# Softmax attention inside an eight-layer model: the bf16 product that opens a score bank, issued half a unit ahead for one head of each pair

## The reference

```python
x = x + _L1_attn_a_ref(_layernorm(x, axis=-1), L1_attn_a_Wq, ...)

q = (x @ Wq.T + bq).reshape(b, s, h, dh)      # b = 1, s = 2048, h = 16, dh = 32
k = (x @ Wk.T + bk).reshape(b, s, h, dh)
v = (x @ Wv.T + bv).reshape(b, s, h, dh)
q = q * jnp.cos(rot)
k = k * jnp.sin(rot)
scores = jnp.einsum('bshd,bthd->bhst', q, k) / np.sqrt(dh).astype(np.float32)
scores = scores * spiral_weight[None, :, None, None]
attn = jax.nn.softmax(scores, axis=-1)
out = jnp.einsum('bhst,bthd->bshd', attn, v).reshape(b, s, d)
return out @ Wo.T + bo
```

## Time and profile before

| | |
|---|---|
| Time, median of 3 runs | 5405.37 us (5400.83 to 5413.63) |
| Profiled execution: its own time | 5397.6 us |
| Its span, first to last instruction | 5395.9 us |
| `attention_heads`, first exponential to the last group's end | 1285 to 2278 us of the span |
| of that, the three quarters which the change touches | 1285 to 2109 us |
| of that, the last quarter | 2109 to 2278 us |
| TensorE over the whole span | 4767.6 us busy, 88% |

### The profile page before, as it was taken

One profiled execution on the slowest core, in us unless ns is written; L12 is line 12 of the kernel. 1 busy time (PEld: TensorE's weight loads), 2 busy tenths in 40 slices (PEclk: granted clock), 3 DMA queues, 4 the chain that ended last, 5 costly groups with the idle time before them and its releaser, 6 DMA issues. The chain is left out here.

```text
span 5395.9 us, 66202 instructions
## 1 busy us (share of the span) xinstructions
PE 4767.6 (88%) x26222; PEld 2548.7 (47%) x26224; DVE 2412.7 (45%) x3331; ACT 1633.7 (30%) x2761; POOL 1532.6 (28%) x953
## 2 busy tenths in 40 slices
PE   7367997899999999967999869999999989589996
PEld 3133433333333333245666536666666654366663
DVE  7854778366666666634222223333333321332222
ACT  5414553212555546702111122222222210121110
POOL 1010000003777764012555401111111110045553
PEclk9688998999999999978999989999999999699998
DMA  2000000100000000044999720000000031459997
GB/s 70 0 2 19 6 0 2 33 0 1 1 1 1 1 1 1 3 165 115 246 253 254 170 76 25 29 30 30 30 22 30 24 105 62 169 163 253 245 254 201
DMA packets 237103, 417.66 MB, mean 77 GB/s; under 512 B 30992, under 2 KB 119056, under 8 KB 236816
## 3 DMA queue, kind: packets, MB, share of 16 engines
q1 hardware_dynamic: 179472, 270.89, 14.5%
q0 software_dynamic: 57344, 142.64, 12.2%
HBM read 297.53 MB, written 115.93 MB: 77 GB/s over the span
## 5 line engine op out<-in xcount | busy, mean ns | idle before, releaser
L2284 PE MATMUL linb_pr_ps<-lin_z,linb_wt 128*128 128x512 f32 x1536 | 679.3, 596 | 16.4 <-POOL linb_slope_own L2254 16.4
L1460 ACT ACTIVATE attc_prob<-attc_ps 128x512 f32<-128x512 f32 x1024 | 548.9, 597 | 438.2 <-PE attc_ps L1371 435.4
L1484 DVE TENSOR_REDUCE attc_peak<-attc_ps 128x2 f32<-128x1024 f32 x384 | 469.7, 1226 | 252.3 <-PE attc_ps L1379 252.3
L1334 POOL TENSOR_TENSOR attc_acc<-attc_acc,attc_prob 128x2048 f32<-128x2048 f32 x120 | 547.9, 4566 | 114.2 <-ACT attc_prob L1460 102.3
L1371 PE MATMUL attc_ps<-att_q,att_k 32*128 32x512 f32 x2048 | 529.2, 616 | 0.0
L2284 PEld LDWEIGHTS linb_pr_ps<-lin_z,linb_wt 128*128 128x128 f32 x1536 | 287.0, 192 | 342.8 <-issue 326.2
L1379 PE MATMUL attc_ps<-att_k,att_q 32*128 32x512 f32 x1536 | 447.1, 659 | 0.0
L2460 DVE SCALAR_TENSOR_TENSOR linb_gated<-linb_osb,linb_norm_w,linb_proj 128x512 f32<-128x512 f32 x64 | 94.4, 1474 | 668.0 <-ACT linb_osb L2387 668.0
L2261 POOL TENSOR_TENSOR linb_sq<-linb_osb 128x512 f32<-128x512 f32 x64 | 70.0, 1094 | 1041.4 <-ACT linb_osb L2387 1041.4
L1009 DVE TENSOR_TENSOR_SCAN ssmb_state<-ssmb_decay,ssmb_bu 128x2048 f32<-128x2048 f32 x64 | 279.8, 4410 | 78.8 <-ACT ssmb_decay L956 78.8
L1392 PE MATMUL attc_ps<-attc_prob,att_v 128*32 128x256 f32 (+1 forms) x3472 | 313.2, 433 | 0.3 <-ACT attc_prob L1460 0.3
(11 more groups left out here) (480 smaller groups left out, 7671.1 us busy)
## 6 DMA issues: line engine op xcount, KB each, us to landing
moe1w_wgu<-in_L_ffn_gate_up_proj SPq DMA_DIRECT2D x32, 1536.0 KB, 10.4
moe2w_wgu<-in_L_ffn_gate_up_proj SPq DMA_DIRECT2D x32, 1536.0 KB, 10.5
moe1w_wd<-in_L_ffn_down_proj SPq DMA_DIRECT2D x32, 512.0 KB, 13.7
gated_features<-linb_gated SPq DMA_DIRECT2D x64, 256.0 KB, 2.3
moe2w_wd<-in_L_ffn_down_proj SPq DMA_DIRECT2D x32, 512.0 KB, 13.6
linc_gt<-gated_features SPq DMA_DIRECT2D x7, 2048.0 KB, 8.2
linb_wt<-in_L_attn_b_qkv_w SPq DMA_DIRECT2D x16, 768.0 KB, 4.7
residual_rows<-residual SPq DMA_DIRECT2D x2, 4096.0 KB, 13.3
```

Of the source, the lines that this page charges most:

```text
L1334: pool.tensor_tensor(acc[:, n % 2, :, :], before, prob[:, U % NP, :, :], ALU.add).then_inc(pool_done, 2 if at == 1 else 1)
L1460: nc.scalar.activation(prob[:, U % NP, h, :], ps[:, n % 3 if at < 0 else at % 6, :], ACT.Exp).then_inc(exp_done, 1)
L1484: V.tensor_reduce(peak[:, w // TT % 2, i % QH, 2 * hp:2 * hp + 2, b], ps[:, bank:bank + 2, :], axis=AX.X, op=ALU.max).then_inc(mx_used, 1)
L2284: last = nc.tensor.matmul(pr_ps[:, use % 2, :], wt[:, b, kind, k, :], z[:, k, t * NB:(t + 1) * NB], start=(k == 0), stop=(k == DT - 1))
```

## The change

`less_max(U, h)` is a new helper that issues the bf16 product of one head and remembers its bank. `scores` calls it only for heads for which that has not been done. The product of head 2 is now issued right after the first half's maxima and ahead of its values; the product of head 0 of the next unit is issued right after the second half's maxima and ahead of its values. Heads 1 and 3 keep their place. Two units of each quarter (those in which `rows` may still be written) and the last quarter have no early product for head 0. The number of instructions stays the same.

```diff
+            opened = {}
+
+            def less_max(U, h):
+                t = U % UNITS // TT
+                own, cols = slice(h * DH, (h + 1) * DH), slice(t * NB, (t + 1) * NB)
+                opened[U, h] = score_bank(QH * U + h)
+                nc.tensor.matmul(ps[:, opened[U, h], :], ones16[own, :], rows[own, cols], start=True, stop=False)
+
             def scores(U, heads):
                 f, w = U // UNITS, U % UNITS
                 t, i = w // TT, w % TT
                 keys, cols = slice(i * P, (i + 1) * P), slice(t * NB, (t + 1) * NB)
-                banks = []
                 for h in heads:
-                    banks.append(score_bank(QH * U + h))
+                    if (U, h) not in opened:
+                        less_max(U, h)
+                for h in heads:
                     own = slice(h * DH, (h + 1) * DH)
-                    nc.tensor.matmul(ps[:, banks[-1], :], ones16[own, :], rows[own, cols], start=True, stop=False)
-                for h, bank in zip(heads, banks):
-                    own = slice(h * DH, (h + 1) * DH)
-                    nc.tensor.matmul(ps[:, bank, :], k[own, f, keys], q[own, f, cols], start=False, stop=True).then_inc(s_done, 1)
+                    nc.tensor.matmul(ps[:, opened[U, h], :], k[own, f, keys], q[own, f, cols], start=False, stop=True).then_inc(s_done, 1)
@@
                 if U < LAST_GROUP:
                     scores(U, (0, 1))
                     maxima(U, "A", (2, 3))
+                    less_max(U, 2)
                     if U >= LAG and (U - LAG) % TT:
                         values(U - LAG, 0)
                     scores(U, (2, 3))
                     maxima(U, "B", (0, 1))
+                    if U + 1 < LAST_GROUP and (U + 1) % UNITS not in (0, UNITS - TT):
+                        less_max(U + 1, 0)
                     if U >= LAG:
                         values(U - LAG, 1 if (U - LAG) % TT else None)
```

## The result

The changed kernel takes 5465.63 us (median of 4 runs, 5461.27 to 5469.64) against 5409.15 us for the kernel before on the same chip. The ratio is 1.0104, with a 95% interval of 1.0092 to 1.0117: it is slower by 1%, some 56 us. The forecast was 5407 us and "no difference". The rival "dearer tail" had the sign, but by a mechanism that did not occur.

A forecast was written before the change was run, and what follows sets the result against it. A loop through TensorE and ScalarE over two halves was taken to set the 3.76 us unit. Group terms +0.22, +0.11, -0.07, -0.1 made +0.17, times twelve +2.0 us: 5407 us, range 5393 to 5425.

The forecast's parts named there:

- no difference: Whole kernel: 5407 us against a median of 5405.4, inside the 11 us distinguishable from no change; chance of same 0.64.
- dearer tail: Rival, switch to values: the bf16 product ahead of it costs more than 0.12; with 0.21, 5434 us; chance 0.23.
- R: Start of the odd head's bf16 product in a half, which waits for the bank read by the even head's previous exponential.
- swallowed by that wait, so it counts nothing: Behind a group's end: TensorE waits 1.97 us for VectorE, so R coming 0.12 earlier changes nothing there.
- Gain side: Each half: even head's k x q may start with R, first exponential 1.16 after it; gain 0.06 per unit at most.
- ScalarE's loop: From R through the even head's k x q and exponential to the next R: 1.81, or 1.89 when also waiting for GpSimd.
- Cost side: Before values in each half: moved product starts at R + 0.98, values at R + 1.29; TensorE's loop grows 1.74 to 1.86.
- The sum over a group: One group of 61.08 us: terms of +0.22, +0.11, -0.07 and -0.1, together +0.17, or +2.0 us over twelve groups.
- hidden product: Rival, mid-group: moved product runs free beside the odd head's second pass; unit 3.70, -0.9 per group, 5394 us; chance 0.17.
- The POOL sums: GpSimd's sums, 602 us of 824 in the three touched quarters, stay behind the loop at 3.75 as at 3.76.
- The list of what would make me wrong: Even exponential not depending on R, early product's bank wait beyond R + 0.98, or halves out of step making GpSimd's sums late.
- my spread: Clock at group ends: shifts may move drops of about 1.1 us in up to 6 groups, 7 us either way.

The follow-up runs named there:

- first run: Changed kernel plus a wait so GpSimd's sum of a group's third unit starts only after VectorE's product of o_raw and tot: 5404.91 us, ratio 1.0002.
- sixth run: Kernel before with only the added wait of GpSimd's sum for VectorE's product of o_raw and tot, no product moved: 5408.77 us, ratio 1.0002.
- fourth: Changed kernel plus the wait on GpSimd's sum, with the even head's k x q issued ahead of the odd head's bf16 product: 5403.25 us, ratio 1.0000.
- seventh run: Kernel before, with the product of o_raw and tot moved to GpSimd and VectorE's reciprocal cut into 8 pieces between later reductions: 5353.27 us, ratio 0.9902.
- fifth run: The fourth run's kernel, with the maxima product on the early product's rows issued first except in a group's third and fourth units: 5376.37 us, ratio 0.9947.

## Why the prediction was wrong

The step that failed is this one, on the stretch behind a group's end: "What TensorE wins or loses in there (R comes 0.12 earlier, the moved product takes it again) is swallowed by that wait, so it counts nothing." The part on R was right to the hundredth: it did come 0.12 earlier. What failed is "swallowed by that wait, so it counts nothing". But R is not only TensorE's business. It releases exponentials, they release GpSimd's sum, and that sum shares a resource with the very VectorE chain that I had named as setting the stretch. I took that chain (reciprocal of 3.35, product, two reductions) for fixed, since its own inputs do not move. Its product became 4.32 us longer, and TensorE's wait at the row turn rose from 1.97 to 6.30 us, 47.6 us over the 11 turns. The order of the two starts, 0.09 us apart, stood in the trace of before (the two lines of "the same place before"), and so did a hint, a sum of 4.97 beside a median of 4.53. I read neither.

The Trainium skill states the rule in "SBUF — State Buffer", section "Who interferes with whom": a VectorE instruction with two SBUF inputs contends with a GpSimd instruction that reads SBUF, the ports that they share are held by an exclusive lock, and the order of issue decides which of the two is blocked. The runs here agree in both directions: product second, 5.01 and 4.72, both done 0.55 after the sum; product first, 0.69, and the sum 4.97 instead of 4.50. The same section says that VectorE instructions with at most one SBUF input don't contend, unless they run in a two-port mode; the reciprocal from 1585.35 took its 3.35, as every one of the 16 does, although a sum of GpSimd ran until 1586.97. The trace after has a closer control than that, an operation of the same kind and size that has one of its inputs in PSUM. It runs beside the sum in front of that one and takes 0.69 us, where all 16 of its kind take 0.68 to 0.69:

```profile
1582.43 4.54 POOL L1334 TENSOR_TENSOR attc_acc<-attc_prob 128x2048 f32<-128x2048 f32 x1 [8.53 <-issue]
1584.62 0.69 DVE L1521 TENSOR_TENSOR attc_tot<-attc_ps,attc_zsum 128x512 f32<-128x512 f32 x1 [2.00 <-PE attc_ps L1413]
```

Point by point:

- Gain side (k x q starts with R, exponential 1.16 or 1.25 after it): held, 1.24 in the half shown (1611.52) and 1.16 in the next (1613.33, R at 1612.17). The next R after 1.89 in first halves held too; the 1.81 of ScalarE's loop is not seen, since TensorE sets second halves.
- Cost side (early product at R + 0.98, values 0.31 behind it, TensorE's half 1.86): held. The rival "dearer tail", on which I had put the whole slower chance of 0.23, is refuted by the 0.31 and by the first and sixth run, which agree.
- The sum over a group, +0.17: too large, if anything. Its own terms give less (thirteen units at 0.01 are 0.13, so +0.13), and in the same way the unit from 3.82 to 3.70 under "hidden product" is worth 0.12, so that rival is 0.84 per group. In the first run the product of o_raw and tot lies at 1576.16 and 1643.84 in two neighbouring groups with full clock between them, 67.68 apart; before, at 1433.70 and 1501.32, 67.62. The change without the collision is worth nothing that can be measured either way, as forecast.
- "The POOL sums (602 us of 824) stay behind the loop": true of their amount, but I asked only whether they become late and not what they exclude when they come early.
- The list of what would make me wrong held the right engine ("GpSimd's sums became late") with the wrong sign: they became early.

The size: 47.6 us of TensorE's added wait is shown, 11 x 4.33, and it agrees with VectorE's added busy time (47.4). The rest goes with the granted clock, and how much that is depends on which execution of before one compares with. In the profiled one of before the clock is low behind 7 of the 11 row turns; in those of the first, fourth and sixth runs, whose wait at the turn is the same, behind 8, 11 and 11. With the early products and the long product it is low behind all 11, and for longer. One such stretch in the profile after:

```profile
1588.70:1592.30 3.60, 0.02 (x4) 0.00 (x0) 3.57 (x1) 0.00 (x0) 3.60 (x1) 1.00 0.00 0
1592.40:1602.40 10.00, 7.38 (x40) 2.81 (x40) 5.65 (x6) 1.88 (x4) 0.79 (x1) 0.50 0.00 0
```

TensorE idles from 1588.72, the clock falls inside this wait to the lower level, 1.2 GHz, and the halves that follow run at it: the bf16 product at 1595.54 takes 0.60 us where the one at 1610.28 takes 0.39. Against the sixth run the three quarters take 55 us more (892 and 837), which is the 56 us of the medians: 47.6 of wait and some 7 of clock. Against the profiled execution of before it is 68 us, of which some 20 go with the clock, but 13 of these lie between two executions with the same short wait. That the clock falls because of the wait is argued from the place, and supported by the seventh run, in which wait and low clock are gone together; no run varies the one alone.

The same rows bear on my spread. I had priced a drop of the clock at 1.1 us in up to 6 groups, 7 us either way. In the sixth run all 11 groups have one, and at 67.6 us for a group at full clock they cost 1.5 to 3.1 us each, so this term was too small. It changes neither the class nor the failed step.

## What to carry to other kernels

Moving a release earlier by a tenth of a microsecond can change an order on any engine downstream. Before calling a wait "cover", list the pairs of instructions that start within that distance of each other near it, and ask for each pair whether VectorE reads two SBUF operands while GpSimd reads SBUF. An order that matters and is held by 0.09 us of luck deserves a semaphore (which cost nothing measurable here) or, better, no pair at all. Putting the short product on GpSimd itself and the long reciprocal off the path gave 1%, more than any reordering of TensorE's products here (0.5% in the fifth run).

## What was not expected of the hardware

- Of VectorE's product and GpSimd's sum, the later is not slowed but held, and the hold is shown as busy time and not as a wait (586.7 against 539.2 us for the same 476 instructions): the product's length is the rest of the sum plus 0.55 us, whether it starts 0.03 or 0.33 us behind (5.01 and 4.72). The other way round the sum pays 0.44 to 0.47 (4.97 against 4.50 to 4.53).
- A memset of 128x256 on VectorE went through in 0.27 us while the sum ran, and the product right behind it did not.
- An f32 pass that starts together with a bf16 product on other rows takes 0.69 instead of 0.59 us, and its successor starts 0.53 instead of 0.43 behind it. Putting it first in the queue did not avoid that: in the fifth run the bf16 product starts 0.07 after the pass at 1582.53, which still takes 0.69. That the bf16 product is the cause is not shown apart from this coincidence.
